# Bias by TensorE and normalising by VectorE in a graph kernel's last three jobs, and products of constants in five waits

## The reference

```python
q, k, v = h @ Wq, h @ Wk, h @ Wv                 # split in 8 heads of 64
e = einsum('ehd,ehd->eh', k[src], q[dst]) / 8    # one score per edge and head
attn = softmax of e over the edges of one target # segment max, sum
a = segment_sum(attn[:, :, None] * v[src], dst)
x = layernorm(h + a @ Wo) * g1 + be1
f = relu(x @ W1 + b1) @ W2 + b2                   # 512 -> 64 -> 512
return layernorm(h + (layernorm(x + f) * g2 + be2))
```

## Time and profile before

| | |
|---|---|
| Median of 3 runs | 696.63 us (696.45 to 697.27) |
| Profiled execution | 701.9 us, span 700.2 us |
| TensorE, VectorE, ScalarE busy | 638.2, 577.0, 533.9 us |
| Last step on VectorE (9:N0.z9) ends | 688.42 us |
| Granted TensorE clock, mean over the span | 0.957 |

### The profile page before, as it was taken

One profiled execution on the slowest core, in us unless ns is written; L12 is line 12 of the kernel. 1 busy time (PEld: TensorE's weight loads), 2 busy tenths in 40 slices (PEclk: granted clock), 3 DMA queues, 4 the chain that ended last, 5 costly groups with the idle time before them and its releaser, 6 DMA issues. The chain is left out here.

```text
span 700.2 us, 10740 instructions
## 1 busy us (share of the span) xinstructions
PE 638.2 (91%) x3450; PEld 487.6 (70%) x3450; DVE 577.0 (82%) x1389; ACT 533.9 (76%) x1151; POOL 398.1 (57%) x363
## 2 busy tenths in 40 slices
PE   3899999999999899999999999999999999967740
PEld 2788877787777677777777777776777777645520
DVE  7658679968898698898889889888898897997672
ACT  1525269978898787988898898879779987997781
POOL 7084354674576655756776575572746374566223
PEclk9999999999999999999999999999999999996755
DMA  7743164555435825663482466446555543655432
GB/s 232 205 114 114 31 149 91 161 118 143 139 97 171 184 67 146 167 147 89 155 187 89 135 176 149 90 157 119 143 127 159 111 105 132 120 119 147 85 66 88
DMA packets 37746, 91.42 MB, mean 131 GB/s; under 512 B 8346, under 2 KB 9642, under 8 KB 37690
## 3 DMA queue, kind: packets, MB, share of 16 engines
q0 software_dynamic: 31536, 82.74, 46.3%
q1 hardware_dynamic: 6154, 8.01, 4.1%
HBM read 71.20 MB, written 20.99 MB: 132 GB/s over the span
## 5 line engine op out<-in xcount | busy, mean ns | idle before, releaser
L530 ACT ACTIVATE squares<-rows,nmean 125x512 bf16<-125x512 f32 x200 | 142.2, 713 | 41.0 <-DVE nmean L857 20.2
L391 POOL DMA_INDIRECT out_dram<-rows,node_idx x40 | 45.9, 1148 | 56.6 <-ACT rows L585 47.1
L445 POOL DMA_DIRECT2D x_rows<-in_L_gnn_ln_b_dram x40 | 53.3, 1375 | 42.2 <-DVE rows L788 28.9
L387 POOL DMA_INDIRECT x_rows<-in_x_dram,node_idx x40 | 45.6, 1140 | 55.6 <-DVE rows L872 41.0
L853 DVE SCALAR_TENSOR_TENSOR rows<-pF,rows 125x512 f32<-125x512 f32 x80 | 51.9, 685 | 24.9 <-PE pF L1027 19.7
L918 PE MATMUL pP<-wo_hi,aT_hi 128*125 128x512 f32 x160 | 66.3, 415 | 0.1
L918 PE MATMUL pP<-xTs_hi,wv_hi 128*128 128x500 f32 x160 | 66.3, 414 | 0.0
L918 PE MATMUL pP<-xTd_hi,wq_hi 128*128 128x500 f32 x160 | 65.6, 410 | 0.0
L918 PE MATMUL pP<-wo_lo,aT_hi 128*125 128x512 f32 x160 | 63.5, 397 | 0.0
L918 PE MATMUL pP<-xTs_hi,wk_hi 128*128 128x500 f32 x160 | 63.5, 397 | 0.0
L918 PE MATMUL pP<-wo_hi,aT_lo 128*125 128x512 f32 x160 | 63.4, 396 | 0.0
(11 more groups left out here) (179 smaller groups left out, 1774.8 us busy)
## 6 DMA issues: line engine op xcount, KB each, us to landing
x_rows<-in_L_gnn_ln_b_dram POOLq DMA_DIRECT2D x40, 512.0 KB
dst_row<-in_dst_dram SPq DMA_DIRECT2D x9, 250.5 KB
q<-in_L_gnn_Wq_dram SPq DMA_DIRECT2D x1, 1024.0 KB, 5.7
rows<-in_L_gnn_Wk_dram SPq DMA_DIRECT2D x1, 1024.0 KB
rows<-in_L_gnn_Wv_dram SPq DMA_DIRECT2D x1, 1024.0 KB, 8.5
x_rows<-in_L_gnn_Wo_dram SPq DMA_DIRECT2D x8, 128.0 KB
xd<-in_x_dram,dst_idx POOLq DMA_INDIRECT x40
xs<-in_x_dram,src_idx POOLq DMA_INDIRECT x40
```

Source lines behind the costliest of these rows:

```text
L387: pool.indirect_dma_start(rows, None, x, bass.IndirectOffsetOnAxis(ap=table[:, column:column + 1].bitcast(U32), axis=0), bounds_check=N - ...
L391: pool.indirect_dma_start(out, bass.IndirectOffsetOnAxis(ap=table[:, column:column + 1].bitcast(U32), axis=0), rows, None, bounds_check=N ...
L445: pool.dma_start(xr_wide[n], bass.AP(tensor=be2.tensor, offset=be2.offset, ap=[[0, P], [0, 2], [1, D]]), accum_op=ALU.add).then_inc(s[f"be ...
L530: ins = act.activation(squares[:, t, :], w[n][:, t, :], ACT.Square, bias=nmean[c][n][:, t:t + 1], accum_out=sq[c][n][:, t:t + 1])
```

## The change

1. For the last three jobs (round 9: E0, E1, N0) the bias is put into the banks by TensorE: step `B9`, two matmuls of the identity and `bias_all`, 125 x 512 each in float32. `F19` writes its sum into the score bank `pS` with `start`, so nothing is zeroed, and `F29` adds onto `B9`'s banks. For E1 they are two of the banks of the big products. ScalarE's `seed` and its copy after relu fall away in these jobs.
2. `norm` of 9:E0 and 9:E1 goes to VectorE (`norm9`, two tensor_scalar of 125 x 512). 9:N0's stays with ScalarE. 9:E0's last normalising goes back from VectorE (`z9`) to ScalarE (`z`).
3. Behind five steps TensorE gets products of constants (`below`, bfloat16, 128 x 512) that nothing reads: 14 behind 8:E1.T, 5 behind 8:E1.F1, 4 behind 9:N1.T, 5 behind 9:O3, 8 behind 9:E0.F19; 36 in all.
4. New due times. The order differs from before in round 0 on GpSimd (`SAVE`, the write of the table `fill_nodes` to memory), then hardly up to the last steps of rounds 5 to 7, and much in rounds 8 and 9.

```diff
-SLOT_PERIOD = {"N0": 7684, "N1": 7682}
+SLOT_PERIOD = {"N0": 7683, "N1": 7685}
...
-E0.T 124763 142872 144266 172069 255824; E0.F1 138155 145181 144555 179712 259103;
+>E0.B9 140397 145236 144577 195268 261664; >E0.F19 138154 145180 144554 215314 261703;
...
-!SAVE -69250; !BIAS -46200; GXD -201076 -32352 122318 122634 124465; GXS -86453 38598 129311 131967 131899;
+!SAVE 15608; !BIAS -46200; GXD -201076 -32352 122318 122662 124531; GXS -86453 38598 129311 130950 129750;
...
+FILLERS = {
+    (8, "E1.T"): 14, (8, "E1.F1"): 5, (9, "N1.T"): 4, (9, "O3"): 5, (9, "E0.F19"): 8
 }
...
+        def hidden(i, slot):
+            n = closing.index((i, slot))
+            return pS[:, R * n:R * n + R]
+
+        def f_banks(i, slot):
+            return pP[0:2] if (i, slot) == closing[1] else pF[::-1]
...
+                    elif what == "F19":
+                        before = job_before(i, slot)
+                        on.wait_ge("f_filled", 2 * nth("pe.F2", before[1], before[0]))
+                        on.wait_ge("h_filled", nth("pe.F1", slot, i))
+                        act.activation(hT[:, :], hidden(i, slot), ACT.Relu, bias=b1_col[:, :]).then_inc(s["h_done"], 1)
...
+                    elif what == "norm9":
+                        on.wait_ge("nb1_done", nth("dve.r1", slot, i))
+                        on.wait_ge(f"out_{slot}", 32 * i)
+                        rows = xr[n] if slot[0] == "N" else w[n]
+                        for t in range(2):
+                            ins = dve.tensor_scalar(w[n][:, t, :], rows[:, t, :], rs[1][n][:, t:t + 1], nb1[n][:, t:t + 1],
+                                                    ALU.mult, ALU.add)
+                        ins.then_inc(s["last_n1_done"], 1)
...
+                    elif what == "B9":
+                        before = closing.index((i, slot))
+                        on.wait_ge("bias_loaded", 16)
+                        on.wait_ge("ident_done", 1)
+                        if before == 1:
+                            on.wait_ge("hx_done", 4 * ROUNDS)
+                        else:
+                            j, old = job_before(i, slot) if before == 0 else closing[0]
+                            on.wait_ge("x2_done", 2 * nth("dve.x2", old, j))
+                        for bank in f_banks(i, slot):
+                            pe.matmul(bank[0:R, :], ident[0:R, 0:R], bias_all[0:R, :], start=True, stop=True)
+                    elif what == "F19":
+                        on.wait_ge("nT_done", 2 * nth("act.T", slot, i))
+                        on.wait_ge("weight_exp", ROUNDS)
+                        if closing.index((i, slot)):
+                            j, old = job_before(i, slot)
+                            on.wait_ge("h_done", nth("act.F1", old, j))
+                        for k in range(KC):
+                            for t in range(2):
+                                ins = pe.matmul(hidden(i, slot)[DFF * t:DFF * t + DFF, :], w1[:, k, :], nT[:, k, R * t:R * t + R],
+                                                start=(k == 0), stop=(k == KC - 1))
+                        ins.then_inc(s["h_filled"], 1)
+                    elif what == "F29":
+                        on.wait_ge("h_done", nth("act.F1", slot, i))
+                        for t in range(2):
+                            pe.matmul(f_banks(i, slot)[t][0:R, :], hT[DFF * t:DFF * t + DFF, :], w2[DFF * t:DFF * t + DFF, :],
+                                      start=False, stop=True, skip_group_check=True).then_inc(s["f_filled"], 1)
...
+                if idle:
+                    on.wait_ge("weight_exp", ROUNDS)
...
+                for _ in range(idle):
+                    pe.matmul(unread[:, :].rearrange("p (a d) -> p a d", a=KC), below[:, :],
+                              below[:, :].rearrange("p (a d) -> p a d", a=1).broadcast_to([P, KC, P]), start=True, stop=True)
```

More of the change, by code:

```diff
@@ L63 @@
[L63 to L66, removed]
+!HQ -299672; !HK -100416; !HV -82111; !HO -39217; TXD0 -126220 -10760 125712 125374 125114;
+TXS0 -98802 24316 131158 131052 131445; Q0 -86658 43928 131621 131047 130453; V0 34194 127287 136963 137053 168307;
@@ new lines @@
+N0.sd 131973 144358 144362 156273 239225; N0.norm 138639 145644 144578 162723 269923;
+<N0.T 144737 146043 145939 164147 321601; >N0.T9 144736 146042 145938 185761 288610;
+>N0.F19 147827 148634 147108 184926 307479; <N0.seed 146713 147667 146603 168921 253680;
+<N0.F1 147828 148635 147109 177714 294217; N0.sq 148296 150099 149101 211191 317209;
+N0.sq3 150400 150451 150214 240448 377777; <N0.z 151393 150665 150731 255450 389678;
+N1.sd 82649 140203 141487 143330 191349; N1.norm 86069 140739 142634 146605 197851;
@@ new lines @@
+N1.T 90041 142589 143122 148648 221748; N1.seed 87282 142429 142185 147389 223957;
+N1.F1 118266 142748 143773 149419 229718; N1.sq 131074 145574 145605 157433 233267;
+N1.sq3 144399 146835 146251 164701 288772; N1.z 146146 148427 148547 171475 312135;
+E0.sd 129457 142196 143068 149879 231097; <E0.norm 130281 142691 143719 151561 210150;
+<E0.T 137146 143033 144061 159011 192960; >E0.T9 137145 143032 144060 163372 243060;
+>E0.F19 139127 145316 144422 157929 256930; <E0.seed 132297 143965 144234 150698 228091;
@@ new lines @@
+<E0.F1 139128 145317 144423 164012 239309; E0.sq 144594 146291 146119 167549 276838;
+E0.sq3 147279 148642 147797 180074 313490; E0.z 148142 149124 149758 197126 330430;
+E1.sd 133115 144208 144278 165298 250301; <E1.norm 142107 144622 144498 178944 229888;
+<E1.T 143387 145695 144586 192985 252860; >E1.T9 143386 145694 144585 219373 261698;
+>E1.F19 144390 146099 145647 194884 280731; <E1.seed 143644 145883 145367 197785 271038;
+<E1.F1 144391 146100 145648 204799 289591; E1.sq 147047 147739 146670 211398 306877;
@@ L281, in graph_attention @@
         place = {key: n for n, key in enumerate(products)}
-        jobs = [(i, step.split(".")[0]) for i, step in pe_steps if step.endswith(".F1")]
+        jobs = [(i, step.split(".")[0]) for i, step in pe_steps if step.endswith((".F1", ".F19"))]
         job = {key: n for n, key in enumerate(jobs)}
+        closing = [(i, step.split(".")[0]) for i, step in pe_steps if step.endswith(".F19")]
+        assert len(closing) == 3 and closing == jobs[-3:]
+        assert all(products[-1] in pe_steps[:pe_steps.index((i, f"{slot}.B9"))] for i, slot in closing[1:])
+        def hidden(i, slot):
[3 more added lines that the diff above has]
+            return pP[0:2] if (i, slot) == closing[1] else pF[::-1]
         def pT_of(i, step, half=0):
@@ L300, in graph_attention @@
                 if "." in step:
-                    slot, what = step.split(".")
+                    slot, what = step.removesuffix("9").split(".")
                     done[what] = done.get(what, 0) + 1
@@ L921, in _ @@
             for i, step in pe_steps:
+                idle = FILLERS.get((i, step), 0)
                 if step == "TURN":
```

196 lines of the change are left out of this document (102 added, 94 removed).

## The result

| | before | after |
|---|---|---|
| Median | 696.54 us (4 runs) | 688.09 us (686.59 to 688.72, 4 runs) |
| Profiled execution, span | 701.9, 700.2 us | 688.38, 686.0 us |
| Same, a second execution of before | 695.25, 693.5 us | |

The ratio of the medians is 0.9882, interval 0.9863 to 0.9902: 8.45 us faster, 1.2%, and clear of the noise. The forecast was 688.2 us, a gain of 8.4. But the two profiles that one would lay side by side first differ by 14.2 us of span. So I profiled the kernel before once more, and compare with that execution.

What follows compares the result with a forecast made beforehand. TensorE, 91% busy, was taken as the bound; from 606 us on it waits, with low clock and chains over four engines. Gains of 4.8 and 3.9 us, less 0.3, gave -8.4: median 688.2 us, range 685.8 to 694.0.

Steps and rivals of the forecast that it cites:

- The axis: Whole kernel: sums made in the profiled execution's time, carried over to the median, 5.3 us below that execution's 701.9.
- Term 1: Start of 9:O0 on TensorE: 8.0 us earlier, with L3 5.5 us earlier and N1.F1 and F2 moved behind O0.
- Term 2: Up to the end of 9:H3 on VectorE: it ends at 649.1 instead of 653.92, gain 4.8 us.
- Term 3: From H3's end to VectorE's last step: 30.6 us instead of 34.5, gain 3.9 us.
- What covers the additions: TensorE's last rounds: B9, 2.1 us each at full clock, and 36 constants, 8.3 us, mostly hidden in waits or behind VectorE.
- Term 4: Round 0, the table's moved write: lands in 3 us at no cost; landing at 8.4 us would cost 4.6 us.
- The tail kept its clock: Rival, TensorE's last jobs: low clock from E0.F29 on, 690 to 692 us, or from E0.B9 on, 695; chance 0.16.
- constants keep nothing and only the order counts: Rival, rounds 8 and 9: clock as before up to 652, tail as forecast, -4 us, 692 to 693; chance 0.07.
- The dearest rival: Rival, 8:E1.T to 9:O1 on TensorE: clock stays low, constants cost double, +11 on -8.4, 699 us; chance 0.05.

Runs made afterwards that it cites:

- E0: Not a follow-up run: one of the kernel's last three jobs in round 9, so it has no edit and no measured median.
- rows_ahead_of_l3: Changed kernel with 8:N0.t and 8:E1.t (with E1.m2) ahead of 9:L2 and 9:L3 on VectorE, as before the change: 706.85 us, ratio 1.0085 to before.
- f_ahead_of_o0: Changed kernel with 9:N1.F1 and 9:N1.F2 ahead of 9:O0 on TensorE, as before the change: 706.87 us, ratio 1.0062 to before.
- table_early: Changed kernel with the table's write (SAVE) at its old place, ahead of the bias and round 1's gathers: 698.78 us, ratio 0.9948 to before.
- no_constants: Changed kernel without its 36 products of constants: 689.03 us, ratio 0.9897 to before.
- after_again: Changed kernel, unchanged, run again on chip 2: 697.33 us, ratio 0.9920 to before.

## Why the prediction was right

- **The axis.** All sums were made in the first profile of before and carried over to the median by its 5.3 us. That was right, and more needed than I knew: that execution had 6.4 us of pauses ahead of 9:K1, which the change doesn't touch.
- **What was luck.** The terms were each within 0.4 us of what the profiles show; that the total agrees to 0.1 us is chance, as the ratio's interval is 1.4 us either way. And the prediction knew nothing of pauses in the changed kernel. The result was taken where its profile shows none; on the other two chips the same kernel gains 5.2 and 3.1 us.
- **Term 1, O0 8.0 us earlier: 7.6.** L3's stretch lost 3.84 us of VectorE's work (52.52 to 48.68; I took 4.0) and 1.3 of its idle (1.5). The rest is N1.F1 and F2 out of the way. rows_ahead_of_l3 and f_ahead_of_o0 show that O0 hangs on both moves, but neither can be undone alone at the price of the term: the other engines' orders assume it. The term's two parts are read from the profiles, not from a run with one of them alone.
- **Term 2, H3 4.8 earlier: 4.7.** O0's start to H3's end was forecast 17.1 us, it takes 16.84. norm9 took 1.00 and 1.14 us (1.19). The estimate of 0.33 us a half from the Trainium skill (VectorE: DVE Perf Modes, the perf-mode tier table with the page's cycle table) is not what this step shows: a half takes 0.54 to 0.68. The prediction went too far in reading such a row as against two elements a cycle: the second half starts 0.46 us behind the first, and no run here parts the time by column from the fixed time of an instruction.
- **Term 3, gain 3.9: 4.1.** Busy forecast 25.0, measured 24.94; idle 5.6, measured 5.44, of it 3.44 for E1.sd (3.2) and 0.78 ahead of N0.r3 (0.9).
- **What covers the additions.** B9 takes 1.88 us at full clock (2.1). F29's new waits are 1.61 and 2.55 us (2 and 2.7), and VectorE waited at most 0.18 us ahead of the x2 of E0, E1 and N0. 14 constants took 3.19 us.
- **Term 4, no cost:** the landing is 3.0 us as assumed, the maximum doesn't wait, and table_early is alike up to 9:K1. The half microsecond in the start of 0:V0 stays open.
- **Rivals.** The tail kept its clock: TensorE's last F29 took 1.23 us, and the 0.82 over the last stretch is from the time after it: up to F29's end it is 0.99. In the other two profiles of the kernel the last F29 is slow, as said above. The rival "constants keep nothing and only the order counts" was put at 692 to 693, and no_constants has 689.0: by this the forecast overrated what low clock ahead of the products costs. The dearest rival, 699 us with the constants running at low clock themselves, no run has tried. Its sum counts T, F1, F2, O0, O1 and 23 constants as slowed; in no_constants F1 ran at full clock, O0 came back to it before its end, and T's loss fell into the wait for L3.
- **What isn't parted.** No run has the new order without `B9`, norm9 and the constants. Its share is what these leave, and since the gains overlap it has no number.

## What to carry to other kernels

Before pricing terms, profile the old kernel twice: 6.4 us of its first profile were that execution's. Price low clock as the waits leave it, not as the sum of slowed instructions: 3.7 us longer ones cost 3.1 us in the profile and 1 to 2 in the medians here. And an order over several engines is one thing: each of two moves undone alone cost 8.4 and 9.5 us, where the whole change brings 3.1 and 5.2 on the same chips.

## What the runs showed that I had not expected

**Pauses of several engines at once.** On chips 2 and 3 the kernels stand still at the same places of the program. TensorE near 233 us and near 592, ScalarE's copy and VectorE's H0 beside it, in after_again:

```profile
232.91 0.65 PE L1022 MATMUL pT<-ident,xd 125*128 125x125 f32 x4 [2.65 <-ACT nT L585]
...
592.12 1.71 PE L1094 MATMUL pF<-nT,w 128*64 128x125 f32 x16 [2.53 <-issue]
...
590.04 0.59 ACT L585 ACTIVATE nT<-pT 128x500 f32<-128x500 f32 x1 [3.77 <-remote]
...
593.06 0.75 DVE L820 SCALAR_TENSOR_TENSOR rows<-pP,is_last,x_rows 125x512 f32<-125x512 f32 x1 [4.68 <-remote]
```

"remote" is a release that the profile can't put down to an instruction of this core. The first profile of before has the first of them:

```profile
232.86 0.66 PE L977 MATMUL pT<-ident,xd 125*128 125x125 f32 x4 [2.67 <-ACT nT L558]
```

GpSimd goes on meanwhile. From 0:V0 to 9:K1 it is 518.2 to 518.8 us in the changed kernel's first profile and the four of chip 1, and 522.0 to 526.1 in the eight on the other chips. What makes them is open, and so is why the changed kernel loses more there (9.2 and 10.3 us against its 688.09) than before does (6.2 and 5.2 against 696.33). The pause near 592 costs the changed kernel 4 us in after_again; whether before has it too can't be said, since before wasn't profiled on those chips.

**Part of the measured time lies outside the span**, 1.7 to 3.5 us by execution, so spans alone don't settle differences of 1 to 2 us.
